# A decoder block's cross attention: all value and sum products of a batch in one row, and x2's turn in another bank

## The chip, the cores and the metric

The kernel runs on one NeuronCore of a Trainium2 chip. The metric is the device time of one execution in microseconds (us). The core has five engines, each with its own in-order instruction list: PE (TensorE, matrix products; PEld is its weight load), DVE (VectorE), ACT (ScalarE), POOL (GpSimd) and SP (SyncE, which issues transfers). They meet only at semaphores. Matrix products land in PSUM, a memory of eight banks.

## The reference

64 batches of 128 tokens with 128 features pass three parts, each followed by a residual sum and a layer norm. The change touches the second, cross attention to 77 context rows of 96 features, with 16 heads of 8:

```python
q = (x @ Wq).reshape(B, N, HEADS, hd).transpose(0, 2, 1, 3)
k = (context @ Wk).reshape(B, M, HEADS, hd).transpose(0, 2, 1, 3)
v = (context @ Wv).reshape(B, M, HEADS, hd).transpose(0, 2, 1, 3)
scores = jnp.einsum('bhid,bhjd->bhij', q, k) * scale
attn = jax.nn.softmax(jnp.where(mask, scores, max_neg), axis=-1)
out = jnp.einsum('bhij,bhjd->bhid', attn, v)
...
x = _layernorm(x + out.reshape(B, N, DIM) @ Wo, axis=-1)
```

Everything is float32.

## The kernel before

The program runs in stages, one behind the other: attention, cross attention (`attend_context`), gathering of expert slots, experts, mixing. In the profile cross attention lies between about 162 and 555 us. It goes in steps `n` from -1 to 67, one batch a step, and is pipelined by hand: in step `n` the scores of batch `n`, the products of batch `n - 2` with the values, the projection of batch `n - 3` and the turn of the finished x2 of batch `n - 4` are done. Each engine's list is written out in the loop `for n in STEPS` of its block, and nothing is reordered.

What a batch goes through:

- `own_keys` (POOL, L797) sets up its keys. `scores` (PE, L550) makes the scores of eight heads a half, in two halves that share the two banks of `psS`; `peak` (DVE, L701) takes their maxima. The second half's scores wait for the first half's peak.
- `turn_max` (PE, L530) turns the negative maxima into `psM`; ACT copies them to `mT` (L676). `turned_scores` (PE, L560) makes the scores again, with the context rows on the partitions, into the four banks of `psP`; `shift` (PE, L568) adds the maxima.
- `exponentials` (ACT, L641) reads `psP` in two halves, two banks each.
- `values` (PE, L579) and `sums` (PE, L585) multiply the exponentials with the values and with ones, both into `psO`, in column tiles of 32. Each comes in two parts, 16 instructions each.
- `invert_sums` (DVE, L720) takes the reciprocal of the sums, `divide` (L730) makes `oT`, `project` (PE, L535) multiplies with Wo into `psM`, `add_residual` (DVE, L708) makes y. Statistics (L710, L715), and `normalise` on POOL (L803 to L808), give x2 in `w.xres`.
- `turn_x2` (PE, L540) turns x2 into `psM`, ACT makes its high part (L679) and `low_part` (DVE, L724) the low one, which the next stage's logits use.

Beside these, every other step has `queries_keys` or `own_values` (PE, into `psM`) for a pair of batches, with their copies on ACT and `split_low` on DVE, and SP stores and reloads the packed queries and keys.

The bank `psM` is shared by five users. `take_bank(reader, count)` lets the next one begin when the reader of the one before is through: the list `held` keeps that semaphore. So after `project`, the next user waits for y (`y_done`).

Of the kernel before, what the change touches and what calls it, by code (L numbers as in the profile page):

```python
# [18 lines left out]
ALU = mybir.AluOpType  # L19
ACT = mybir.ActivationFunctionType  # L20
# [7 lines left out]
B, S, D = 64, 128, 128  # L28
TOKENS = B * S
J, JP, CD = 77, 78, 96  # L30
# [25 lines left out]
def reach(eng, sem, value):  # L56

    if not isinstance(value, int) or value > 0:
        eng.wait_ge(sem, value)  # L59
# [366 lines left out]
def attend_context(nc, io, w):  # L426
# [4 lines left out]
    with ExitStack() as ctx:  # L431
        st = Store(nc, ctx, "cross")
# [24 lines left out]
        qk_made, high_ready, low_ready, t_made = w.qk_made, w.high_ready, w.low_ready, w.t_made  # L457
        kd_ready, v_made, vd_ready = (st.sem(n) for n in ("kd_ready", "v_made", "vd_ready"))

        s_made, mx_ready, m_made, mT_ready, e_ready, av_made, rs_ready, oT_ready = (  # L460
            st.sem(n) for n in ("s_made", "mx_ready", "m_made", "mT_ready", "e_ready", "av_made", "rs_ready",
                                "oT_ready"))
# [6 lines left out]
        block = ctx.enter_context(nc.Block())  # L469
        PACKS = 6 * 16  # L470
        STEPS = range(-1, B + 4)

        def is_batch(n):
            return 0 <= n < B

        def projected(n):
            return [(n + 4) // 2] if n % 2 == 0 and 0 <= n + 4 < B else []
# [8 lines left out]
        def tokens(n):  # L486
            return slice(n * 128, n * 128 + 128)
# [18 lines left out]
        def _(pe):  # L506
            held = []

            def take_bank(reader, count):
                for sem, value in held:  # L510
                    pe.wait_ge(sem, value)
                held[:] = [(reader, count)]
# [23 lines left out]

            def turn_x2(n):
                pe.wait_ge(x2_kept, n + 1)
                take_bank(xl_ready, n + 1)
                pe.transpose(psM[:, 0:128], w.xres[:, tokens(n)], w.ident).then_inc(xT_made, 1)  # L540

            def scores(n, half):
                r, b = n // 2, n % 2
# [10 lines left out]
            def turned_scores(n):  # L554
                r, b = n // 2, n % 2
                reach(pe, e_ready, n)
                for q in range(4):
                    for i in range(4):
                        row = pack[r % 2][32 * i:32 * i + 32, q, :]
                        pe.matmul(psP[:, i, q, :], row[:, 256 + b * JP:256 + b * JP + J], row[:, b * 128:b * 128 + 128],  # L560
                                  start=(q == 0), stop=False, skip_group_check=True)
# [10 lines left out]
            def values(n, part):  # L572
                if part == 0:
                    pe.wait_ge(vd_ready, n // 2 + 1)
                    pe.wait_ge(e_ready, n + 1)
                    reach(pe, oT_ready, n)
                for i in range(2 * part, 2 * part + 2):
                    for q in range(4):
                        pe.matmul(psO[32 * q:32 * q + 32, 0, :], vd[n // 2 % 3][:, 4 * (n % 2) + q, 32 * i:32 * i + 32],  # L579
                                  pT[n % 2][:, i, q, :], start=(i == 0), stop=(i == 3), skip_group_check=True)  # L580
# [15 lines left out]

            for n in STEPS:
                if n == 2:
                    pe.wait_ge(od_set, 2)
                if is_batch(n):  # L600
                    scores(n, 0)
                for r in projected(n):
                    queries_keys(r)
                for r in valued(n):
                    own_values(r)
                if is_batch(n - 2):
                    values(n - 2, 0)
                if is_batch(n):
                    scores(n, 1)
                if is_batch(n - 2):  # L610
                    values(n - 2, 1)
                if is_batch(n - 3):
                    project(n - 3)
                if is_batch(n - 2):
                    sums(n - 2, 0)
                if is_batch(n):
                    turn_max(n)
                    turned_scores(n)
                if is_batch(n - 4):
                    turn_x2(n - 4)  # L620
                if is_batch(n - 2):
                    sums(n - 2, 1)
                if n == 0:
                    pe.wait_ge(consts_set, 1)
                if is_batch(n):
                    shift(n)
                if n == B:
                    turn_weights(0)
                    turn_weights(1)
                if n == B + 1:  # L630
                    turn_weights(2)
                    turn_weights(3)

        @block.scalar
        def _(act):
            def exponentials(n, half):
                if half == 0:
                    act.wait_ge(t_made, n + 1)
                    reach(act, av_made, n - 1)
                hs = slice(2 * half, 2 * half + 2)  # L640
                ins = act.activation(pT[n % 2][0:J, hs, :, :], psP[:, hs, :, :], ACT.Exp)  # L641
                if half == 1:
                    ins.then_inc(e_ready, 1)

            def weights_high(c):
                b = slice(c * 512, (c + 1) * 512)
                act.wait_ge(w_made, c + 1)
                act.copy(w.w1h[:, b], psW[:, b]).then_inc(wh_done, 1)

            for n in STEPS:  # L650
                if n in (1, 2):
                    act.wait_ge(pT_set, n)
                if n == B + 1:
                    weights_high(0)
                    weights_high(1)
                if n == B + 2:
                    weights_high(2)
                    weights_high(3)
                if is_batch(n - 1):
                    exponentials(n - 1, 0)  # L660
                for r in projected(n):
                    act.wait_ge(qk_made, r + 1)
                    reach(act, stored, 16 * r)
                    act.copy(qk[:, 0, :], psM[:, 0:WIDE]).then_inc(high_ready, 1)
                for r in valued(n):
                    act.wait_ge(v_made, r + 1)
                    act.wait_ge(vd_clear, min(r, 2) + 1)
                    reach(act, av_made, 2 * r - 4)
                    act.copy(blocks(vd[r % 3][0:J]), psM[0:J, 0:256].rearrange("j (c h e) -> j c h e", c=8, h=4))\
                        .then_inc(vd_ready, 1)  # L670
                if is_batch(n - 1):
                    exponentials(n - 1, 1)
                if is_batch(n):
                    act.wait_ge(m_made, n + 1)
                    reach(act, t_made, n)
                    act.copy(mT[:], psM[:, 0:128]).then_inc(mT_ready, 1)  # L676
                if is_batch(n - 4):
                    act.wait_ge(xT_made, n - 3)
                    act.copy(w.xh[0:127, tokens(n - 4)], psM[0:127, 0:128]).then_inc(xh_ready, 1)  # L679

        @block.vector
        def _(dve):
# [9 lines left out]
            def split_low(r):  # L692
                dve.wait_ge(high_ready, r + 1)
                dve.tensor_tensor(qk[:, 1, :], psM[:, 0:WIDE], qk[:, 0, :], ALU.subtract)\
                    .then_inc(low_ready, 1)
# [25 lines left out]

            def low_part(n):
                dve.wait_ge(xh_ready, n + 1)
                dve.tensor_tensor(w.xl[0:127, tokens(n)], psM[0:127, 0:128], w.xh[0:127, tokens(n)], ALU.subtract)\  # L724
                    .then_inc(xl_ready, 1)

            def divide(n):
# [16 lines left out]
            for n in STEPS:  # L744
                if n < 2:
                    clear_values(n + 1)
                if n == B + 3:
                    weights_low(2)
                if is_batch(n):
                    peak(n, 0)  # L750
                for r in projected(n):
                    split_low(r)
                if is_batch(n):
                    peak(n, 1)
                if is_batch(n - 3):
                    add_residual(n - 3)
                    aggregate(n - 3)
                if is_batch(n - 4):
                    low_part(n - 4)
                if n == B + 2:  # L760
                    weights_low(1)
                if is_batch(n - 2):
                    invert_sums(n - 2)
                    divide(n - 2)
                if n == B - 1:

                    dve.wait_ge(qk_made, PAIRS)
                    dve.wait_ge(w.phi_loaded, 32)
                    dve.tensor_copy(w.diff[:, :, 127], w.bias[:])
                    differences((0, 1))  # L770
                if n == B:
                    differences((2, 3))
                if n == B + 1:
                    weights_low(0)
                if n == B + 3:
                    weights_low(3)
# [694 lines left out]
```

## Time and profile before

| | |
|---|---|
| median of 3 runs | 1484.61 us (1484.57 to 1485.5) |
| span of the profiled execution | 1482.3 us, so the median lies 2.3 us above it |
| PE, PEld busy over the span | 92%, 74% |
| DVE, ACT, POOL busy over the span | 81%, 59%, 79% |
| mean granted TensorE clock | 0.976 of 2.4 GHz |

A profile is one execution. Busy shares are means over stages with different limits, and the ends of matmuls are modelled, so a PE that shows as busy can be waiting for part of that time. What a change in one stage is worth must be read from that stage's timeline.

### The profile page before, as it was taken

What the parts mean: (1) busy time and instruction counts of PE and PEld (TensorE: products, weight loads), DVE (VectorE), ACT (ScalarE), POOL (GpSimd) and SP (SyncE); (2) the same over time, 40 slices, a digit from 0 to 9 for tenths busy, and PEclk for the clock granted to TensorE, in tenths of its full rate; (3) what the DMA queues carried; (4) which work ended last, traced back from release to release, by engine and by line L of the source; (5) the groups of instructions that cost most, each with busy time, mean ns of one, the idle gap of its engine ahead of it and who ended that gap; (6) DMA issues with size and microseconds to landing.
All of it is one profiled execution on the core that took longest, in us unless ns stands there. A gap on an engine that the chain in (4) does not pass through costs nothing. (4 is left out here: it accounts for less than half of the span.)

```text
span 1482.3 us, 34966 instructions
## 1 busy us (share of the span) xinstructions
PE 1369.5 (92%) x12862; PEld 1092.1 (74%) x12862; DVE 1197.3 (81%) x2379; ACT 873.4 (59%) x1542; POOL 1167.6 (79%) x1036
## 2 busy tenths in 40 slices
PE   4765699999999977999999999996999999999998
PEld 3554566666666655777777777765999999999997
DVE  5998467766776766888888888886999999999996
ACT  2777444544544534777777777764566666666665
POOL 6344466666666645999999999995999999999997
PEclk8999599999999998999999999999999999999999
DMA  5110343333333305222222222212233233232231
GB/s 157 38 35 27 94 123 94 99 103 105 98 94 94 92 20 171 79 79 79 79 79 78 79 79 78 79 71 69 69 93 88 79 92 87 79 93 86 80 93 29
DMA packets 77195, 123.81 MB, mean 84 GB/s; under 512 B 8354, under 2 KB 45795, under 8 KB 77027
## 3 DMA queue, kind: packets, MB, share of 16 engines
q1 hardware_dynamic: 75426, 117.16, 25.2%
q0 software_dynamic: 1088, 4.19, 1.0%
q8 instruction: 104, 1.70, 0.5%
q14 instruction: 65, 0.52, 0.1%
q10 hardware_dynamic: 512, 0.23, 0.1%
HBM read 70.28 MB, written 51.27 MB: 82 GB/s over the span
## 5 line engine op out<-in xcount | busy, mean ns | idle before, releaser
L971 POOL TENSOR_TENSOR gather_d<-gather_e,gather_rinv 128x1024 f32<-128x1024 f32 x128 | 244.9, 1913 | 44.6 <-DVE gather_rinv L950 44.6
L1230 POOL TENSOR_TENSOR mix_c<-mix_e,mix_rinv 128x1024 f32<-128x1024 f32 x128 | 240.9, 1903 | 17.4 <-DVE mix_rinv L1218 13.4
L1298 PEld LDWEIGHTS last_Y<-kept_phi,last_cT 128*128 128x128 f32 x2048 | 248.3, 192 | 7.1
L1298 PE MATMUL last_Y<-kept_phi,last_cT 128*128 128x128 f32 x2048 | 249.1, 275 | 0.0
L1314 ACT COPY last_cT<-last_T 128x1024 f32<-128x1024 f32 x128 | 128.4, 1003 | 128.8 <-PE last_T L1305 128.8
L1215 DVE TENSOR_REDUCE mix_sums<-mix_e 128x16 f32<-128x1024 f32 x128 | 155.9, 1218 | 32.8 <-ACT mix_e L1189 32.6
L946 DVE TENSOR_REDUCE gather_rsum<-gather_e 128x32 f32<-128x1024 f32 x128 | 156.1, 1220 | 26.2 <-ACT gather_e L919 26.2
L797 POOL TENSOR_TENSOR cross_kd<-first_pack,kept_consts 128x624 fp32r<-128x624 f32 x128 | 155.5, 1236 | 18.9 <-DMA first_pack<-first_halves 12.5
L965 POOL TENSOR_TENSOR gather_dl<-gather_d,gather_dh 128x512 fp32r<-128x512 f32 x128 | 166.2, 1299 | 0.0
L641 ACT ACTIVATE cross_pT<-cross_P 77x1024 f32<-77x1024 f32 x128 | 130.3, 1021 | 49.7 <-PE cross_P L568 49.7
L908 ACT COPY gather_keep<-gather_L 128x256 f32<-128x256 f32 x256 | 94.7, 370 | 104.2 <-PE gather_L L882 97.2
L1305 PE MATMUL last_T<-kept_consts,mix_c 128*128 128x128 f32 x1024 | 133.8, 274 | 3.2 <-POOL mix_c L1230 1.2
L919 ACT ACTIVATE gather_e<-gather_L 128x1024 f32<-128x1024 f32 x128 | 131.1, 1025 | 7.8 <-PE gather_L L889 0.3
L896 PE MATMUL slots_X<-gather_d,kept_xres 128*128 128x512 f32 x256 | 130.7, 592 | 0.0
L1223 POOL TENSOR_TENSOR mix_less<-mix_read,mix_high 128x1024 f32<-128x1024 f32 x64 | 122.5, 1914 | 6.5 <-DVE mix_high L1205 3.7
L701 DVE TENSOR_REDUCE cross_mx<-cross_S 128x8 fp32r<-128x624 f32 x128 | 102.9, 804 | 28.7 <-PE cross_S L550 28.6
L1305 PEld LDWEIGHTS last_T<-kept_consts,mix_c 128*128 128x128 f32 x1024 | 113.8, 141 | 4.4 <-issue 2.5
L940 DVE TENSOR_REDUCE gather_mx<-gather_L 128x16 fp32r<-128x512 f32 x128 | 88.5, 691 | 31.7 <-PE gather_L L882 22.9
L901 PE MATMUL slots_X<-gather_dh,gather_x2h 128*128 128x512 f32 x128 | 101.0, 789 | 2.9 <-DVE gather_x2l L956 1.5
L803 POOL TENSOR_TENSOR cross_veps<-cross_mv,kept_eps 128x1 f32<-128x1 f32 x64 | 12.1, 190 | 110.0 <-DVE cross_mv L715 110.0
L931 ACT CAST gather_dh<-gather_d 128x512 fp32r<-128x512 f32 x128 | 79.5, 621 | 31.6 <-PE slots_X L903 20.1
L882 PE MATMUL gather_L<-over_w1h,kept_xh 128*128 128x512 f32 x256 | 82.0, 402 | 10.6 <-ACT gather_e L919 9.1
(195 smaller groups left out, 3166.2 us busy)
## 6 DMA issues: line engine op xcount, KB each, us to landing
kept_logits<-gather_keep SPq DMA_DIRECT2D x128, 256.0 KB, 2.0
mix_read<-kept_logits SPq DMA_DIRECT2D x64, 512.0 KB, 3.7
first_halves<-first_qk SPq DMA_DIRECT2D x32, 412.0 KB, 3.7
first_pack<-first_halves SPq DMA_DIRECT2D x64, 128.0 KB
first_pack<-first_halves SPq DMA_DIRECT2D x32, 206.0 KB
first_pack<-first_halves SPq DMA_DIRECT2D x64, 78.0 KB
attn_xTg<-in_xT SPq DMA_DIRECT2D x16, 256.0 KB, 2.8
kept_xres<-in_x POOLq DMA_DIRECT2D x4, 1024.0 KB, 12.8
```

What stands on the lines that cost most here:

```text
L641: ins = act.activation(pT[n % 2][0:J, hs, :, :], psP[:, hs, :, :], ACT.Exp)
L797: pool.tensor_tensor(kd[n % 2][:, q], keys[:, q].to_broadcast([128, 2, 4, JP]), w.own.unsqueeze(1).unsqueeze(3).to_broadcast([128, 2, 4, J ...
L896: pe.matmul(psX[:, 2 * j + 1, :], w.xres[:, rows(u)], dd[u % 4][:, 1, :], start=first, stop=last)\
L919: act.activation(e[u % 2][:], psL[u % 2][:].rearrange("p i (n s) -> p i n s", n=16), ACT.Exp)\
L946: dve.tensor_reduce(rsum[u % 2][:].rearrange("p (i n) -> p i n", i=2), e[u % 2][:], X, ALU.add)\
L965: pool.tensor_tensor(dl[u % 2][:], dd[u % 4][:, 0, :], dh[u % 2][:], ALU.subtract).then_inc(dl_ready, 1)
L971: pool.tensor_tensor(dd[u % 4][:].rearrange("p i (n s) -> p i n s", n=16), e[u % 2][:], rinv[u % 2][:].rearrange("p (i n) -> p i n", i=2). ...
L1215: dve.tensor_reduce(self.sums[u % 2][:], self.e[u % 2][:], X, ALU.add).then_inc(self.sum_done, 1)
L1230: pool.tensor_tensor(self.cc[u % 2][:], self.e[u % 2][:], self.rinv[u % 2][:].unsqueeze(2).to_broadcast([128, 16, EXPERTS]), ALU.mult)\
L1298: ins = pe.matmul(psY[t % 2][:, 0:128], cT[u % 2][:, c, :], w.yk[:, 8 * (u % 2) + c, :], start=(u % 2 == 0 and c == 0), stop=(u % 2 == 1 a ...
L1305: ins = pe.transpose(psT[:, c, :], mix.cc[u % 2][:, 2 * c:2 * c + 2, :], w.ident)
L1314: act.copy(cT[u % 2][:], psT[:]).then_inc(cT_ready, 1)
```

## The change

On PE, the two parts of the values and the two parts of the sums of batch `n - 2`, which stood at four places of a step, are issued in one row behind the second scores. The turn of x2 goes to the front of the step, ahead of the second scores. It writes the first bank of `psP` and not `psM`, for all but the last four batches, and waits for the first half of the exponentials (a new semaphore `e_low`); the turned scores, which write that bank, wait for the low part of x2. On ACT, x2's high part goes ahead of the second half of the exponentials. On DVE, the low part goes ahead of the second peak, and reciprocal and divide go ahead of the residual sum.

```diff
--- before.py
+++ after.py
@@ -457,6 +457,7 @@
         qk_made, high_ready, low_ready, t_made = w.qk_made, w.high_ready, w.low_ready, w.t_made
         kd_ready, v_made, vd_ready = (st.sem(n) for n in ("kd_ready", "v_made", "vd_ready"))
 
+        e_low = st.sem("e_low")
         s_made, mx_ready, m_made, mT_ready, e_ready, av_made, rs_ready, oT_ready = (
             st.sem(n) for n in ("s_made", "mx_ready", "m_made", "mT_ready", "e_ready", "av_made", "rs_ready",
                                 "oT_ready"))
@@ -469,9 +470,13 @@
         block = ctx.enter_context(nc.Block())
         PACKS = 6 * 16
         STEPS = range(-1, B + 4)
+        SHARED = B - 4
 
         def is_batch(n):
             return 0 <= n < B
+
+        def x2_turned(n):
+            return banks[:, 0, 0, :] if n < SHARED else psM[:, 0:128]
 
         def projected(n):
             return [(n + 4) // 2] if n % 2 == 0 and 0 <= n + 4 < B else []
@@ -536,8 +541,11 @@
 
             def turn_x2(n):
                 pe.wait_ge(x2_kept, n + 1)
-                take_bank(xl_ready, n + 1)
-                pe.transpose(psM[:, 0:128], w.xres[:, tokens(n)], w.ident).then_inc(xT_made, 1)
+                if n < SHARED:
+                    pe.wait_ge(e_low, n + 4)
+                else:
+                    take_bank(xl_ready, n + 1)
+                pe.transpose(x2_turned(n), w.xres[:, tokens(n)], w.ident).then_inc(xT_made, 1)
 
             def scores(n, half):
                 r, b = n // 2, n % 2
@@ -554,6 +562,7 @@
             def turned_scores(n):
                 r, b = n // 2, n % 2
                 reach(pe, e_ready, n)
+                reach(pe, xl_ready, n - 3)
                 for q in range(4):
                     for i in range(4):
                         row = pack[r % 2][32 * i:32 * i + 32, q, :]
@@ -603,23 +612,20 @@
                     queries_keys(r)
                 for r in valued(n):
                     own_values(r)
-                if is_batch(n - 2):
-                    values(n - 2, 0)
+                if is_batch(n - 4):
+                    turn_x2(n - 4)
                 if is_batch(n):
                     scores(n, 1)
                 if is_batch(n - 2):
+                    values(n - 2, 0)
                     values(n - 2, 1)
+                    sums(n - 2, 0)
+                    sums(n - 2, 1)
                 if is_batch(n - 3):
                     project(n - 3)
-                if is_batch(n - 2):
-                    sums(n - 2, 0)
                 if is_batch(n):
                     turn_max(n)
                     turned_scores(n)
-                if is_batch(n - 4):
-                    turn_x2(n - 4)
-                if is_batch(n - 2):
-                    sums(n - 2, 1)
                 if n == 0:
                     pe.wait_ge(consts_set, 1)
                 if is_batch(n):
@@ -638,9 +644,8 @@
                     act.wait_ge(t_made, n + 1)
                     reach(act, av_made, n - 1)
                 hs = slice(2 * half, 2 * half + 2)
-                ins = act.activation(pT[n % 2][0:J, hs, :, :], psP[:, hs, :, :], ACT.Exp)
-                if half == 1:
-                    ins.then_inc(e_ready, 1)
+                act.activation(pT[n % 2][0:J, hs, :, :], psP[:, hs, :, :], ACT.Exp)\
+                    .then_inc(e_ready if half == 1 else e_low, 1)
 
             def weights_high(c):
                 b = slice(c * 512, (c + 1) * 512)
@@ -668,15 +673,15 @@
                     reach(act, av_made, 2 * r - 4)
                     act.copy(blocks(vd[r % 3][0:J]), psM[0:J, 0:256].rearrange("j (c h e) -> j c h e", c=8, h=4))\
                         .then_inc(vd_ready, 1)
+                if is_batch(n - 4):
+                    act.wait_ge(xT_made, n - 3)
+                    act.copy(w.xh[0:127, tokens(n - 4)], x2_turned(n - 4)[0:127]).then_inc(xh_ready, 1)
                 if is_batch(n - 1):
                     exponentials(n - 1, 1)
                 if is_batch(n):
                     act.wait_ge(m_made, n + 1)
                     reach(act, t_made, n)
                     act.copy(mT[:], psM[:, 0:128]).then_inc(mT_ready, 1)
-                if is_batch(n - 4):
-                    act.wait_ge(xT_made, n - 3)
-                    act.copy(w.xh[0:127, tokens(n - 4)], psM[0:127, 0:128]).then_inc(xh_ready, 1)
 
         @block.vector
         def _(dve):
@@ -721,7 +726,7 @@
 
             def low_part(n):
                 dve.wait_ge(xh_ready, n + 1)
-                dve.tensor_tensor(w.xl[0:127, tokens(n)], psM[0:127, 0:128], w.xh[0:127, tokens(n)], ALU.subtract)\
+                dve.tensor_tensor(w.xl[0:127, tokens(n)], x2_turned(n)[0:127], w.xh[0:127, tokens(n)], ALU.subtract)\
                     .then_inc(xl_ready, 1)
 
             def divide(n):
@@ -750,18 +755,18 @@
                     peak(n, 0)
                 for r in projected(n):
                     split_low(r)
+                if is_batch(n - 4):
+                    low_part(n - 4)
                 if is_batch(n):
                     peak(n, 1)
+                if is_batch(n - 2):
+                    invert_sums(n - 2)
+                    divide(n - 2)
                 if is_batch(n - 3):
                     add_residual(n - 3)
                     aggregate(n - 3)
-                if is_batch(n - 4):
-                    low_part(n - 4)
                 if n == B + 2:
                     weights_low(1)
-                if is_batch(n - 2):
-                    invert_sums(n - 2)
-                    divide(n - 2)
                 if n == B - 1:
 
                     dve.wait_ge(qk_made, PAIRS)
```

## Rows read from the trace of the kernel before

**Rows 1.** Stretches: busy us (and instructions) by engine, granted clock, DMA share, GB/s

```profile
100.00:120.00 20.00, 13.09 (x90) 10.71 (x91) 19.02 (x70) 16.42 (x55) 8.64 (x9) 1.00 0.14 39
181.80:540.31 358.51, 348.44 (x6580) 243.38 (x6576) 249.46 (x576) 172.24 (x301) 238.09 (x303) 1.00 0.33 97
```

**Rows 2.** Timeline (start, us, engine): first and last regular shift

```profile
181.80 0.36 PEld L568 LDWEIGHTS cross_P<-cross_mT,cross_pick 32*77 32x77 f32 x16 [0.20 <-issue]
...
540.31 0.35 PEld L568 LDWEIGHTS cross_P<-cross_mT,cross_pick 32*77 32x77 f32 x16 [0.20 <-issue]
```

**Rows 3.** Timeline of one regular step, selected; idle time and releaser in brackets

```profile
451.50 0.38 PEld L585 LDWEIGHTS cross_O<-cross_pT,cross_od 128*32 128x32 f32 x16
...
452.08 0.36 PEld L568 LDWEIGHTS cross_P<-cross_mT,cross_pick 32*77 32x77 f32 x16 [0.20 <-issue]
...
452.22 0.96 DVE L720 RECIPROCAL cross_rs<-cross_O 128x128 f32<-128x128 f32 x1
452.51 0.30 PEld L550 LDWEIGHTS cross_S<-cross_kd,first_pack 128*128 128x128 f32 x2
...
452.63 1.02 ACT L641 ACTIVATE cross_pT<-cross_P 77x1024 f32<-77x1024 f32 x1 [0.75 <-PE cross_P L568]
...
453.21 0.29 DVE L730 TENSOR_TENSOR cross_oT<-cross_O,cross_rs 128x128 f32<-128x128 f32 x1
453.42 0.80 DVE L701 TENSOR_REDUCE cross_mx<-cross_S 128x8 fp32r<-128x624 f32 x1
...
453.62 0.41 PEld L579 LDWEIGHTS cross_O<-cross_pT,cross_vd 128*32 128x32 f32 x16 [0.35 <-issue]
...
454.33 0.30 PEld L550 LDWEIGHTS cross_S<-cross_kd,first_pack 128*128 128x128 f32 x2 [0.31 <-issue]
...
454.82 0.65 PE L579 MATMUL cross_O<-cross_pT,cross_vd 128*32 128x128 f32 x16
454.93 0.81 DVE L701 TENSOR_REDUCE cross_mx<-cross_S 128x8 fp32r<-128x624 f32 x1 [0.71 <-PE cross_S L550]
455.39 0.30 PEld L535 LDWEIGHTS cross_M<-first_xo,cross_oT 128*128 128x128 f32 x2 [0.20 <-issue]
...
455.92 0.29 DVE L708 TENSOR_TENSOR cross_y<-cross_M,kept_xres 128x128 f32<-128x128 f32 x1 [0.18 <-PE cross_M L535]
...
456.38 0.19 PEld L530 LDWEIGHTS cross_M<-kept_neg_ident,cross_mx 128*128 128x128 f32 x1 [0.20 <-issue]
...
456.64 0.36 PEld L560 LDWEIGHTS cross_P<-first_pack 32*77 32x77 f32 x16
...
456.75 0.27 ACT L676 CAST cross_mT<-cross_M 128x128 fp32r<-128x128 f32 x1 [1.92 <-PE cross_M L530]
...
457.13 0.14 PEld L540 LDWEIGHTS cross_M<-kept_consts,kept_xres 128*128 128x128 f32 x1
...
457.39 0.38 PEld L585 LDWEIGHTS cross_O<-cross_pT,cross_od 128*32 128x32 f32 x16
...
457.80 0.29 DVE L724 TENSOR_TENSOR kept_xl<-cross_M,kept_xh 127x128 fp32r<-127x128 f32 x1 [1.03 <-ACT kept_xh L679]
```

**Rows 4.** Timeline of the last steps and the next stage's first logits

```profile
541.84 0.84 PEld L579 LDWEIGHTS cross_O<-cross_pT,cross_vd 128*32 128x32 f32 x32 [1.18 <-issue]
541.87 1.08 PE L579 MATMUL cross_O<-cross_pT,cross_vd 128*32 128x128 f32 x32 [1.07 <-DVE cross_oT L730]
542.88 0.30 PEld L535 LDWEIGHTS cross_M<-first_xo,cross_oT 128*128 128x128 f32 x2 [0.20 <-issue]
...
551.12 0.29 DVE L708 TENSOR_TENSOR cross_y<-cross_M,kept_xres 128x128 f32<-128x128 f32 x1
...
551.52 0.14 PEld L540 LDWEIGHTS cross_M<-kept_consts,kept_xres 128*128 128x128 f32 x1 [0.64 <-issue]
...
553.82 0.14 PEld L540 LDWEIGHTS cross_M<-kept_consts,kept_xres 128*128 128x128 f32 x1 [2.16 <-POOL kept_xres L808]
...
555.65 0.50 PEld L882 LDWEIGHTS gather_L<-over_w1h,kept_xh 128*128 128x128 f32 x2 [1.69 <-issue]
```

## The prediction

> **What bounds the kernel now.** I looked for the stretch that the diff touches. The table by stretch gives it [rows 1]: from the first regular step to the last (181.80 to 540.31 us) TensorE is busy 348.44 of 358.51 us, at a granted clock of 1.00 (2.4 GHz), while VectorE has 249.46, GpSimd 238.09 and ScalarE 172.24. That looks like a TensorE bound, but the ends of matmuls are modelled. So I read the timeline next. The same instruction, the shift (L568), begins at 181.80 in step 2 and at 540.31 in step 63 [rows 2]: 358.51 / 61 = 5.877 us a step. A single step, from the sums at 451.50 to those at 457.39 [rows 3], takes 5.89, the same as this mean over steps whose lists differ (own_values in one, queries_keys in the next). That points to a loop of waits and not to the length of TensorE's list.
>
> The loop stands in the timeline of one step [rows 3]; follow the starts. Second half of the sums (451.50) to reciprocal (452.22): 0.72. Reciprocal to divide (453.21): 0.99. Divide to first peak (453.42): 0.21. Peak to second scores (454.33), which need the score bank that this peak reads: 0.91. Second scores, values, project, sums, turn of the maximum, turned scores, turn of x2, and the second half of the sums again (457.39): 0.49 + 0.57 + 0.99 + 0.26 + 0.49 + 0.26. Together 5.89, the period. So now the batch's reciprocal and divide stand between the sums and the next step's peak, and TensorE fills most of the time but waits a little for them.
>
> Note what does not stand in this loop: the residual sum y (455.92). It runs while the first half of the sums is on TensorE, so that the turn of the maximum, which needs y to have read bank M, finds the bank free at 456.38.
>
> **The change, part by part.** I write M for the start of the turn of the maximum and V for the start of the row of products.
>
> (a) *One row instead of four groups.* It removes no instruction. A group of 16 instructions costs 0.57 from start to the next kind (454.82 to 455.39), with 0.20 of idle weight load at its edge [rows 3]. Where the trace has 32 of them in a row, they take 1.08 against 0.65 for 16 (L579, matmul rows) [rows 3, 4], so a further 16 cost 0.43. Four groups of 0.57 are 2.28; one row is 0.57 + 3 x 0.43 = 1.86. TensorE's list gets 0.42 us shorter a step. Bounds for a further 16: 0.43 from the matmul rows, and 0.47 from the starts of the same run and of the project behind it (541.84 to 542.88, less 0.57); above, no saving at all, 0.57.
>
> The rule that supports this is in the Trainium skill, TensorEngine Tiling (Array Packing), "Tiling Modes": changing the tiling mode, not just the tile, drains the engine. The trace agrees, with the 0.20 us of idle weight load at such edges. By that rule alone fewer changes of mode make the kernel faster, to about 1451 us (rival 2); by VectorE's order, which comes next, it is 1544.
>
> (b) *The new order on VectorE.* It is now: first peak, split_low, low part, second peak, reciprocal, divide, then y of the batch before, stats. TensorE's order is: row, project, turn of the maximum. Project takes bank M, and the turn of the maximum may take it only when y has read it. But y is queued behind the reciprocal and the divide, and these wait for the end of the row. The reciprocal starts 0.72 after a group of 16 starts, so after a row V + 0.72 + 3 x 0.43 = V + 2.01. Then 0.99 to the divide, 0.21 to y (as the divide's follower starts now), 0.29 for y, and 0.11 from the end of a y to TensorE, as in the tail (551.12 + 0.29 to 551.52) [rows 4]. M = V + 3.61. TensorE has by then been done with the row and with project since V + 1.86 + 0.42 = V + 2.28. So it stands for 1.33 us, and turned scores, shift, and everything of the next step stand queued behind it. This is a wait that the kernel before does not have.
>
> (c) *x2's turn in the turned scores' first bank.* It now waits for the first half of the exponentials (e_low) and not for bank M. From M: the copy of the maximum on ScalarE starts 0.37 later and takes 0.27, plus 0.11 to TensorE: shift at M + 0.75 (turned scores, 0.26 + 0.49, are through at the same time). Shift to exponential: 452.08 to 452.63, 0.55; it takes 1.02; plus 0.11: the turn of x2 at M + 2.43. With 0.26 for itself (457.13 to 457.39), second scores at M + 2.69. The other road there goes by the peak: shift to first scores 0.43, scores to peak 0.60 (as from 454.33 to 454.93), peak 0.80, 0.11: M + 2.69. Both roads are equally long, so (c) costs nothing beside the peak; without that cover it would cost up to the difference to own_values' end (first scores to values is 1.11 at most, so M + 2.29), 0.4 us. The high and low copies come earlier in ScalarE's and VectorE's lists: x2's turn to the end of its low part is 0.96 (457.13 to 457.80 + 0.29), so M + 3.4. The next reciprocal is at M + 5.2, and in between lie only the second peak (0.8) and, every other step, split_low; no cost. The second exponential moves behind x's high copy, by 0.27, and is needed only at the next turned scores: no cost.
>
> (d) *Closing the loop.* Second scores to the next row: 0.49. V' = M + 3.18. Period = 3.61 + 3.18 = 6.79 us, against 5.877: +0.91 a step. GpSimd, DMA queues: own_keys and normalise sit where they were, the stores and packs of SP still hang on the shift; with longer steps each has more room. No cost.
>
> (e) *The ends.* Steps -1 to 1 hold nothing that moves. Step 2 has the row and no project, so no wait; it gains about 0.2. Steps 3 to 63 are 61 periods: 61 x 0.91 = 55.5. Behind the last shift, x2's turn now stands ahead of the row and of the project, so each of the last steps waits for the whole chain y, stats, GpSimd's normalise, which takes 2.70 from y to the turn of x2 (551.12 to 553.82) [rows 4]. From the shift S of step 63: y(60) at S - 1.15, turn at 1.55, row 1.81, reciprocal 3.82, y(61) 5.02, turn 7.72, row 7.98, reciprocal 9.99, y(62) 11.19, turn 13.89, low part done 14.85, project 15.0, y(63) 15.5, turn 18.2, next stage 20.0 (1.83 on, as from 553.82 to 555.65). Before it is 15.34 (540.31 to 555.65). +4.7.
>
> Sum: -0.2 + 55.5 + 4.7 = +60. What follows is not touched and is shifted as a whole. The profiled execution spans 1482.3, so 1542.3; the median of the runs lies 2.3 above the span, which gives 1544.6. I say 1544.
>
> **Rivals.**
>
> 1. *The row is not cheaper than its parts* (0.57 a group): reciprocal 0.42 later, period 7.21, 61 x 1.33 + 5 = +86, 1571. With 0.47 instead of 0.43 it is +0.12 a step, 1552. Against: the run of 32 in the tail.
>
> 2. *The other side: TensorE's list decides, y comes in time.* TensorE's starts in the new order: 0.26 + 0.49 + 0.43 + 1.11 + 0.26 + 0.49 + 1.86 + 0.42 = 5.32, so -0.56 a step, -34, about 1451. It holds if y is done within V + 2.28, that is if it is not behind reciprocal and divide, 1.2 us. The list puts it there, so I give this little. (It is the outcome that the Trainium skill's rule on drains, TensorEngine Tiling (Array Packing), "Tiling Modes", would lead one to expect.)
>
> 3. *The change does not show*: the new wait would have to be eaten by other slack to within 0.05 us a step. TensorE, busy 97% by the table, has no such slack on the road from M to V', which is a chain of ScalarE, VectorE and TensorE without gaps. 1485.
>
> 4. *The granted clock falls* to 1.2 GHz, because TensorE now stands 1.3 in 6.8 us. Against: a stretch of the attention stage keeps 1.00 with TensorE busy 13.09 of 20 us [rows 1], a smaller share than in the new step. At half the rate the row's 1.72 us (4 x 0.43) come again, and as an estimate 0.8 for the other matmuls on the loop (half of the 0.49 + 0.43 + 0.26 + 0.43 that they take there): 61 x 2.5 = 154 more, 1698.
>
> **How the numbers follow.** Forecast as worked out 0.86, alone between 1534 and 1557 (period 6.65 to 6.95, the latencies of 0.11 and the 0.43 each being good to some hundredths). Rival 1 with no saving 0.05, rival 2 0.04, rival 3 0.02, rival 4 0.03. About 0.2%, 3 us, is what a measurement of this kernel can tell. Slower 0.94, same 0.02, faster 0.04. The range for 8 in 10 is 1530 to 1562; it takes in the bound of 0.47 with something more.
>
> **What would show it.** After: the turn of the maximum begins about 6.8 us after its predecessor and each time about 0.11 after the end of y; y follows the divide at once; TensorE's longest idle time of a step, some 1.3 us, is put down to VectorE's y, ahead of L530; the reciprocal starts 2.0 after the row; the stage from the first to the last shift takes some 414 us in place of 358.5, with clock 1.00. If the period is 5.3 and y comes ahead of the reciprocal's end, I am wrong in (b); if x2's turn or second scores wait clearly beyond M + 2.7, in (c); if the reciprocal starts 2.4 after V, in (a).

## The result and the profile after

The changed kernel takes 1559.65 us (median of 4 runs, 1556.75 to 1562.27) against 1485.05 us: a ratio of 1.0503, 95% interval 1.0489 to 1.0517. It is 75 us slower; 59 had been forecast, and 1559.65 lies near the upper end of the range.

The profiled execution spans 1557.7 us, 75.4 more than before. The changed lines have moved by a few numbers: L535 is now the turn of the maximum, L577 the shift, L588 the values, L594 the sums, L540 project, L713 y, L725 the reciprocal, L548 x2's turn, L558 the scores. First the table by stretch (busy us and instructions of PE, PEld, DVE, ACT, POOL, then granted clock, DMA share, GB/s): from the turn of the maximum in step 2 to that in step 63, then the tail, then one long step.

```profile
179.02:601.86 422.84, 333.51 (x6579) 264.21 (x6576) 242.77 (x576) 169.26 (x301) 236.74 (x300) 0.96 0.27 82
601.86:627.82 25.96, 14.29 (x187) 11.39 (x188) 10.92 (x32) 5.51 (x11) 7.63 (x12) 0.67 0.00 1
...
480.18:489.30 9.12, 8.05 (x108) 6.42 (x108) 3.82 (x10) 2.74 (x5) 3.94 (x5) 0.63 0.13 47
```

Over the same 61 steps, counted there from shift to shift, TensorE was all but full before [rows 1]; now it is busy 333.51 of 422.84 us, and its clock is no longer 1.00. The timeline has the place: first and last regular shift, one regular step from the turn of the maximum to the next, the values of a long step, and the next stage's first logits.

```profile
179.71 0.35 PEld L577 LDWEIGHTS cross_P<-cross_mT,cross_pick 32*77 32x77 f32 x16
...
453.26 0.19 PEld L535 LDWEIGHTS cross_M<-kept_neg_ident,cross_mx 128*128 128x128 f32 x1 [1.44 <-issue]
...
453.62 0.27 ACT L684 CAST cross_mT<-cross_M 128x128 fp32r<-128x128 f32 x1 [3.12 <-PE cross_M L535]
...
453.94 0.35 PEld L577 LDWEIGHTS cross_P<-cross_mT,cross_pick 32*77 32x77 f32 x16
...
454.49 1.02 ACT L647 ACTIVATE cross_pT<-cross_P 77x1024 f32<-77x1024 f32 x1 [0.60 <-PE cross_P L577]
...
454.70 0.80 POOL L813 TENSOR_SCALAR kept_xres<-cross_y,cross_mv,cross_rstd 128x128 f32<-128x128 f32 x1
...
454.95 0.81 DVE L706 TENSOR_REDUCE cross_mx<-cross_S 128x8 fp32r<-128x624 f32 x1 [1.26 <-PE cross_S L558]
...
455.62 0.14 PEld L548 LDWEIGHTS cross_P<-kept_consts,kept_xres 128*128 128x128 f32 x1 [0.50 <-POOL kept_xres L813]
...
455.88 0.30 PEld L558 LDWEIGHTS cross_S<-cross_kd,first_pack 128*128 128x128 f32 x2
...
456.36 0.81 PEld L588 LDWEIGHTS cross_O<-cross_pT,cross_vd 128*32 128x32 f32 x32 [0.19 <-issue]
456.37 1.08 PE L588 MATMUL cross_O<-cross_pT,cross_vd 128*32 128x128 f32 x32
...
458.25 0.30 PEld L540 LDWEIGHTS cross_M<-first_xo,cross_oT 128*128 128x128 f32 x2 [0.20 <-issue]
...
458.39 0.96 DVE L725 RECIPROCAL cross_rs<-cross_O 128x128 f32<-128x128 f32 x1 [1.09 <-PE cross_O L594]
459.38 0.29 DVE L735 TENSOR_TENSOR cross_oT<-cross_O,cross_rs 128x128 f32<-128x128 f32 x1
459.59 0.28 DVE L713 TENSOR_TENSOR cross_y<-cross_M,kept_xres 128x128 f32<-128x128 f32 x1
...
459.98 0.19 PEld L535 LDWEIGHTS cross_M<-kept_neg_ident,cross_mx 128*128 128x128 f32 x1 [1.44 <-issue]
...
484.00 1.94 PE L588 MATMUL cross_O<-cross_pT,cross_vd 128*32 128x128 f32 x32
...
602.53 0.36 PEld L577 LDWEIGHTS cross_P<-cross_mT,cross_pick 32*77 32x77 f32 x16
...
627.82 0.50 PEld L887 LDWEIGHTS gather_L<-over_w1h,kept_xh 128*128 128x128 f32 x2 [1.79 <-issue]
```

The reader is to see three things. The turn of the maximum (459.98) begins 0.11 us after the end of y (459.59 + 0.28), with 1.44 us of idle weight load ahead of it, while project had begun at 458.25. Y begins behind the divide (459.38), the divide behind the reciprocal (458.39). In the kernel before [rows 3], y lay between the two halves of the sums and the reciprocal behind it. Last, the 32 value products of the step with the turn at 480.18 take 1.94 us (484.00), those of the regular step 1.08 (456.37): the long step ran in part at the lower of the two clock levels, with 0.63 on the mean.

Where the 75.4 us are, from the starts of the shift and of the next stage:

| part | before | after | difference |
|---|---|---|---|
| to the shift of step 2 | 181.80 | 179.71 | -2.1 |
| 61 steps, before at their mean of 5.877, after at their median of 6.73 | 358.5 | 410.5 | +52.0 |
| what some steps take above that | 0 | 12.3 | +12.3 |
| last shift to the next stage's logits | 15.34 | 25.29 | +10.0 |
| the stages behind | 926.65 | 929.88 | +3.2 |

### The profile page after: what moved, and what is told of

Same layout as the page of the kernel before. It is cut to its first block and busy times, and to the rows that moved or that the text cites. A ratio compares the mean times of both kernels' runs of the same rounds, so it can differ in the third digit from the quotient of the medians.

```text
span 1557.7 us, 35026 instructions
## 1 busy us (share of the span) xinstructions
PE 1362.8 (87%) x12862; PEld 1121.5 (72%) x12862; DVE 1188.6 (76%) x2379; ACT 870.1 (56%) x1542; POOL 1168.4 (75%) x1036
## 5 line engine op out<-in xcount | busy, mean ns | idle before, releaser
L684 ACT CAST cross_mT<-cross_M 128x128 fp32r<-128x128 f32 x64 | 17.0, 265 | 203.8 <-PE cross_M L535 203.8
L725 DVE RECIPROCAL cross_rs<-cross_O 128x128 f32<-128x128 f32 x64 | 61.3, 958 | 67.6 <-PE cross_O L594 67.6
```

## The experiments

Step lengths are the distances between the starts of the turn of the maximum. "Long" are steps above 7.4 us.

```
kernel           median step   what steps take above it   time us    ratio to before (95%)
before           5.88          -0.5                       1485.05    1
after            6.73          12.3 (8 long)              1559.65    1.0503 (1.0489 to 1.0517)
e1_y_first       5.93           6.0 (4 long)              1499.12    1.0097 (1.0068 to 1.0125)
e2_project_mid   5.55           0.1                       1465.97    0.9873 (0.9858 to 0.9887)
e3_fill          6.73           3.6 (2 long)              1548.67    1.0428 (1.0412 to 1.0444)
e4_x2_back       7.05 to 8.66, in turn                    1601.81    1.0772 (1.0737 to 1.0807)
e5_x2_alone      5.56           0.6                       1467.87    0.9893 (0.9877 to 0.9910)
e6_fill10        6.73           0.7 (0 long)              1545.21    1.0410 (1.0392 to 1.0428)
e7_ahead         5.29           3.2 (1 long)              1451.75    0.9779 (0.9760 to 0.9797)
e8_row_alone     5.88          -1.0                       1484.78    0.9999 (0.9990 to 1.0008)
```

**e1_y_first: y ahead of the reciprocal.** One edit to the changed kernel, on VectorE:

```diff
-                if is_batch(n - 2):
-                    invert_sums(n - 2)
-                    divide(n - 2)
                 if is_batch(n - 3):
                     add_residual(n - 3)
                     aggregate(n - 3)
+                if is_batch(n - 2):
+                    invert_sums(n - 2)
+                    divide(n - 2)
```

> One edit to the changed kernel: on VectorE the residual sum y and its statistics stand ahead of reciprocal and divide again. Theory A (y queued behind reciprocal and divide is the new wait): y starts 2.4 us after the row, with project, in place of 3.2; the turn of the maximum 2.8 after the row in place of 3.6; the period falls from 6.73 to about 5.9 us and the total to some 1495 us. Theory B (the row itself, or x2's turn in the other bank, is what makes the step longer): the period stays near 6.7 us and the total near 1558 us.

Measured: 1499.12 us, 5.93 us a step. In its timeline the row begins at 450.62, y at 453.03, 2.41 behind it, and the turn of the maximum at 453.44, 2.82 behind it.

```profile
450.62 0.81 PEld L588 LDWEIGHTS cross_O<-cross_pT,cross_vd 128*32 128x32 f32 x32 [0.19 <-issue]
...
452.50 0.30 PEld L540 LDWEIGHTS cross_M<-first_xo,cross_oT 128*128 128x128 f32 x2 [0.20 <-issue]
...
453.03 0.29 DVE L713 TENSOR_TENSOR cross_y<-cross_M,kept_xres 128x128 f32<-128x128 f32 x1 [1.09 <-PE cross_M L540]
...
453.44 0.19 PEld L535 LDWEIGHTS cross_M<-kept_neg_ident,cross_mx 128*128 128x128 f32 x1 [0.64 <-issue]
...
453.79 0.94 DVE L725 RECIPROCAL cross_rs<-cross_O 128x128 f32<-128x128 f32 x1
```

The reciprocal (453.79) now comes after the turn of the maximum. Theory A holds: the place of the residual sum in VectorE's list was worth 60 of the 75 us, the long steps that went with it among them.

**e2_project_mid: y under the sums.** As e1, and on TensorE:

```diff
                     values(n - 2, 1)
-                    sums(n - 2, 0)
-                    sums(n - 2, 1)
                 if is_batch(n - 3):
                     project(n - 3)
+                if is_batch(n - 2):
+                    sums(n - 2, 0)
+                    sums(n - 2, 1)
```

> As e1, and project goes between the values and the sums of the row, so that y is read while the sums run. Theory A: no wait for y is left; the turn of the maximum comes 2.4 us after the row's start, right behind the sums; period about 5.5 us, total about 1472 us, faster than the kernel before. Theory B: near 6.7 us a step still, total near 1560 us.

Measured: 1465.97 us, 5.55 us a step, 1.3% faster than the kernel before. Its timeline, from one row of values to the next:

```profile
449.58 0.81 PEld L588 LDWEIGHTS cross_O<-cross_pT,cross_vd 128*32 128x32 f32 x32 [0.19 <-issue]
...
450.59 0.30 PEld L540 LDWEIGHTS cross_M<-first_xo,cross_oT 128*128 128x128 f32 x2 [0.20 <-issue]
...
451.00 0.81 PEld L594 LDWEIGHTS cross_O<-cross_pT,cross_od 128*32 128x32 f32 x32
...
451.12 0.29 DVE L714 TENSOR_TENSOR cross_y<-cross_M,kept_xres 128x128 f32<-128x128 f32 x1 [0.61 <-PE cross_M L540]
...
452.02 0.19 PEld L535 LDWEIGHTS cross_M<-kept_neg_ident,cross_mx 128*128 128x128 f32 x1 [0.20 <-issue]
...
452.15 0.96 DVE L726 RECIPROCAL cross_rs<-cross_O 128x128 f32<-128x128 f32 x1 [0.20 <-PE cross_O L594]
...
455.13 0.81 PEld L588 LDWEIGHTS cross_O<-cross_pT,cross_vd 128*32 128x32 f32 x32 [0.19 <-issue]
```

Project starts at 450.59, y at 451.12 while the sums (451.00) run, and the turn of the maximum at 452.02, 2.44 behind the row's start, finds bank M free.

**e4_x2_back, e5_x2_alone, e8_row_alone: the two halves of the change.** E4 undoes x2's move in the changed kernel. E5 makes this move alone in the kernel before. E8 has the row alone, in e2's order, that is with project between values and sums, so that the row is two groups of 32.

```diff
# e5: x2's turn in the kernel before
+                if is_batch(n - 4) and n - 4 < SHARED:
+                    turn_x2(n - 4)
                 if is_batch(n):
                     scores(n, 1)
...
                     turned_scores(n)
-                if is_batch(n - 4):
+                if n - 4 >= SHARED and is_batch(n - 4):
                     turn_x2(n - 4)
# e4 and e8: x2's turn back in bank M, behind the turned scores
-                if is_batch(n - 4):
-                    turn_x2(n - 4)
                 if is_batch(n):
                     scores(n, 1)
...
                     turned_scores(n)
+                if is_batch(n - 4):
+                    turn_x2(n - 4)
```

> The changed kernel with x2's turn alone undone: bank M, behind the turned scores, its copies last in ScalarE's and VectorE's lists; the row stays. If x2's move costs nothing, as predicted, and only takes x2's turn (0.26 us) from between turned scores and shift: the period grows to about 7.0 us, total about 1577 us. If x2's move is part of what made the kernel slower: the period falls below 6.7 us, total under 1555 us.

Measured: 1601.81 us. For most of the stage the steps come in turn, as about 8.6, 8.05, 7.05 and 7.05 us; those at full clock are 7.05, 0.32 longer than in the changed kernel. So x2's move saves 0.32 us a step there. The rest of the loss goes with the clock: 0.87 over the regular steps, the lowest of all these kernels.

```profile
180.00:647.04 467.04, 367.67 (x6474) 290.02 (x6471) 243.71 (x566) 169.66 (x296) 235.10 (x297) 0.87 0.25 74
```

> The kernel before with x2's move alone: its turn goes into the turned scores' first bank, between the first values and the second scores, with its copies earlier on ScalarE and VectorE; values and sums stay in four groups, VectorE keeps y ahead of the reciprocal. If the loop sums, reciprocal, divide, peak, second scores sets the step, as read from the trace of before, it loses x2's 0.26 us between turned scores and the second sums and may get back 0.12 before the second scores: period 5.6 to 5.75 us, total 1469 to 1477 us. If x2's move costs as much as it saves: 1485 us.

Measured: 1467.87 us, 5.56 us a step. x2's move alone makes the kernel before 1.1% faster, 0.32 us a step, a little more than expected. In its timeline the loop of the kernel before is still there, without x2's 0.26 us, and the second half of the sums starts 0.43 behind the turned scores (451.36 to 451.79), where x2's turn had started 0.49 behind them.

> The row without x2's move, and without the wait for y: values, project, sums behind both scores; y ahead of reciprocal and divide; x2's turn in bank M behind the turned scores, as in the kernel before, only its low part is made last on VectorE. With e5_x2_alone it tells the two halves of the change apart. If the row's saving of some 0.4 us of TensorE is hidden, because the loop of waits and not TensorE's list sets the step: e2's 5.55 us plus the 0.32 us that x2's move was worth in e4, 5.85 to 5.9 us a step, total 1482 to 1488 us. If the row saves its 0.4 us: about 5.5 us a step, total 1463 us.

Measured: 1484.78 us, 5.88 us a step, ratio 0.9999 (0.9990 to 1.0008). Together the three give a table of four: neither 5.88, x2's move alone 5.56, the row alone 5.88, both (e2) 5.55. So the row, taken by itself and without the wait for y, gains nothing. The timeline of e8, from one row to the next, shows what became of it:

```profile
446.36 0.81 PEld L587 LDWEIGHTS cross_O<-cross_pT,cross_vd 128*32 128x32 f32 x32 [0.18 <-issue]
...
447.37 0.30 PEld L540 LDWEIGHTS cross_M<-first_xo,cross_oT 128*128 128x128 f32 x2 [0.20 <-issue]
...
447.79 0.81 PEld L593 LDWEIGHTS cross_O<-cross_pT,cross_od 128*32 128x32 f32 x32
...
448.80 0.19 PEld L535 LDWEIGHTS cross_M<-kept_neg_ident,cross_mx 128*128 128x128 f32 x1 [0.20 <-issue]
...
449.93 0.29 DVE L735 TENSOR_TENSOR cross_oT<-cross_O,cross_rs 128x128 f32<-128x128 f32 x1
...
450.23 0.30 PEld L558 LDWEIGHTS cross_S<-cross_kd,first_pack 128*128 128x128 f32 x2
...
450.82 0.81 DVE L706 TENSOR_REDUCE cross_mx<-cross_S 128x8 fp32r<-128x624 f32 x1 [0.32 <-PE cross_S L558]
...
451.75 0.30 PEld L558 LDWEIGHTS cross_S<-cross_kd,first_pack 128*128 128x128 f32 x2 [0.76 <-issue]
...
452.23 0.81 PEld L587 LDWEIGHTS cross_O<-cross_pT,cross_vd 128*32 128x32 f32 x32 [0.19 <-issue]
```

The values take 1.01 us (446.36 to 447.37) and the sums 1.01 (447.79 to 448.80), 2.02 us for what was four groups of 0.57 [rows 3]: TensorE's list is 0.26 us shorter. (The row in one piece, in the changed kernel, takes 1.89: 456.36 to 458.25.) But the step now has another loop than the kernel before. The divide is through at 450.22 (449.93 + 0.29), and the first peak (450.82) waits for the first scores (450.23) and no longer for the divide. From row to row the loop is: values, project and sums 2.44, from the turn of the maximum over turned scores, x2's turn and shift to the first scores 1.43, to the peak 0.59, to the second scores 0.93, to the row 0.48, together 5.87. So the new order takes reciprocal and divide off the loop, and lays the first half of the values, the shift and the first scores on it. The shorter list counts on this loop, but the longer road uses it up. That the old loop and the new one come to the same 5.88 us is a coincidence, and so is 5.56 beside 5.55: in e2 it is the new loop without x2's turn, in e5 the old one without it.

**e3_fill and e6_fill10: the clock.** The changed kernel, with work added where TensorE waits for y (six products in e3, ten in e6; their output is overwritten):

```diff
                     project(n - 3)
+                    if is_batch(n):
+                        pe.wait_ge(mx_ready, 2 * n + 2)
+                        for q in (0, 1, 0, 1, 0, 1):
+                            pe.matmul(psS[:, q, 0:HW], w.neg_ident[:], pick[:].rearrange("p q t -> p (q t)"),
+                                      start=True, stop=True)
```

> The changed kernel with six added products of constants (128x128 by 128x312, some 0.9 us) into the score banks in the time in which TensorE stands for y. They are extra work that the next scores overwrite. Theory C (the ten steps that take 7 to 9 us in place of 6.73, and the slow last steps, come from the granted clock falling because TensorE stands 1.4 us in each step): the period stays 6.73 us, the long steps are gone, the clock stays 1.00 between the first and last step, and the total falls by 12 to 18 us to about 1543 us. Theory D (they come from something else, a transfer or the batches' pairs): the long steps stay, total 1560 us or more.

> As e3_fill, with ten added products instead of six, which fill the wait for y up to some 0.15 us. Theory C (the clock falls because TensorE stands in each step): the long steps, ten without filling and four with six products, go to none or one; period still 6.73 us; total near 1545 us. Theory D: the number of long steps does not follow the filling and stays at four or more.

Measured: 1548.67 and 1545.21 us, with the same 6.73 us a step. The long steps go from eight to two to none. Two of the ten that the expectations count, of 6.96 us, stay in all three kernels 128 to 129 us apart, at a clock of 1.00 (255.42:262.38 in the changed kernel), so they have another cause, which stays open. The regular steps of e3, by stretch:

```profile
180.03:594.15 414.12, 375.83 (x6945) 303.87 (x6941) 242.56 (x576) 169.52 (x301) 237.03 (x300) 0.99 0.28 84
```

and of e6:

```profile
181.19:592.39 411.20, 398.87 (x7189) 336.06 (x7185) 242.60 (x576) 169.21 (x301) 236.81 (x300) 1.00 0.28 85
```

More work on TensorE, and 14 us less time: theory C holds for the long steps. The products cost nothing since they stand where TensorE stood anyway.

**e7_ahead: one step further.** As e2, with x2's turn beside project, its copies behind the second exponentials and behind the statistics, and

```diff
-                if is_batch(n):
-                    scores(n, 0)
...
                     sums(n - 2, 1)
+                if is_batch(n + 1):
+                    scores(n + 1, 0)
                 if is_batch(n):
                     turn_max(n)
```

> As e2_project_mid, with two more edits: x2's turn stands beside project between values and sums, and the next batch's first scores are issued behind the sums, ahead of the turn of the maximum, so that their peak and the exponentials are off the road to the second scores. If TensorE's own list bounds e2 by now (starts of its pieces add up to 5.4 to 5.6 us), the period falls only to about 5.45 and the total to about 1460 us. If e2 is still bound by the road over exponentials, peak and normalise (3.1 us from the turn of the maximum to the row), the period falls to 5.2 or less, total 1445 us.

Measured: 1451.75 us, 2.2% faster than the kernel before and the fastest here; 5.29 us a step lies between the two expectations, nearer to the second. In its timeline

```profile
449.62 0.96 DVE L726 RECIPROCAL cross_rs<-cross_O 128x128 f32<-128x128 f32 x1
...
450.61 0.29 DVE L736 TENSOR_TENSOR cross_oT<-cross_O,cross_rs 128x128 f32<-128x128 f32 x1
450.82 0.80 DVE L707 TENSOR_REDUCE cross_mx<-cross_S 128x8 fp32r<-128x624 f32 x1
...
451.73 0.30 PEld L558 LDWEIGHTS cross_S<-cross_kd,first_pack 128*128 128x128 f32 x2 [0.43 <-issue]
...
452.21 0.81 PEld L588 LDWEIGHTS cross_O<-cross_pT,cross_vd 128*32 128x32 f32 x32 [0.18 <-issue]
```

reciprocal, divide and first peak stand end to end, and the second scores (451.73) still wait for the peak (450.82 + 0.80), 0.43 us of idle weight load: reciprocal, divide and peak are on the loop again, as in the kernel before [rows 3]. That reading comes from this one timeline; no run took it apart further. The one long step (from 197.47, 9.21 us at a mean clock of 0.84) is of another kind: in it ScalarE's copy of the queries and keys waits 2.59 us for a store, and project has 2.82 us of idle weight load ahead of it.

## Why the prediction was right, and by how much it was off

The wait that the prediction named is there, and the total lies within its range. That it does is in part luck: the range was meant for some hundredths of a us in each step, and there the steps came out 3.5 us below the forecast (52.0 against 55.5). The total lies above the forecast because of the long steps and the tail, where the clock fell, and the sum had that at nothing.

**(b), the new wait, was right.** Shown by e1 and e2. Its terms, forecast and measured from the timeline of after: row to reciprocal 2.01, 2.03; to divide 0.99, 0.99; to y 0.21, 0.21; y's start to the turn of the maximum 0.40, 0.39.

**(c) and (d), the road back to the row, were right to some hundredths.** Turn of the maximum to shift 0.75, measured 0.68; to x2's turn 2.43, measured 2.36; x2's turn to the second scores 0.26, 0.26; these to the row 0.49, 0.48. The period comes to 6.72, against 6.79. One road was left out of (c): x2's turn also waits for GpSimd's normalise of the y of the step before, which ends at 455.50 (454.70 + 0.80), while the first half of the exponentials ends at 455.51. It was a tie, so the sum did not suffer. What (c) called free was more than that: e4 and e5 show that x2's move is a gain of 0.32 us a step, in the changed kernel and in the one before. The prediction had taken x2's 0.26 us off the road to the shift, but never set it down as a gain of its own.

**(a), the row, was right in its size.** 1.89 us, forecast 1.86. The trace agrees with the rule on drains in the Trainium skill, TensorEngine Tiling (Array Packing), "Tiling Modes": with fewer changes of mode TensorE's list is 0.39 us shorter a step (four times 0.57, less 1.89). In the changed kernel this counts, since the reciprocal waits for the row's end. Against the kernel before, the row is worth nothing, as e8 shows, because its order makes a loop just as long. That also answers rival 2: e2 and e8 have no wait for y, and neither comes to the 5.32 us that TensorE's list alone would give. Rivals 1 and 3 fell with the row's 1.89 us and the ratio of 1.0503.

**(e), the ends, was mis-sized.** Forecast +4.7 behind the last shift, measured +10.0. The chain y, normalise, x2's turn is there, but two of its links are longer than in the steps from which they were taken. The rows below are from the tail of the changed kernel, the first a stretch as in the table of the result.

```profile
605.33:608.90 3.57, 3.57 (x65) 2.99 (x65) 0.29 (x1) 1.18 (x2) 0.00 (x0) 0.50 0.02 5
...
602.37 0.63 POOL L808 TENSOR_TENSOR cross_veps<-cross_mv,kept_eps 128x1 f32<-128x1 f32 x1 [7.36 <-DVE cross_mv L720]
...
603.08 0.89 POOL L811 TENSOR_TENSOR cross_rstd<-cross_veps,kept_neg_half 128x1 f32<-128x1 f32 x1
...
605.33 1.94 PE L588 MATMUL cross_O<-cross_pT,cross_vd 128*32 128x128 f32 x32
...
609.04 0.96 DVE L725 RECIPROCAL cross_rs<-cross_O 128x128 f32<-128x128 f32 x1 [3.01 <-PE cross_O L594]
```

The first row runs at a clock of 0.50, and the reciprocal starts 3.71 us behind it (605.33 to 609.04); the second, at 0.57, takes 3.33 (613.87 to 617.20). The forecast had 2.01 for each, so 3.0 us of the missing 5.3 are here. GpSimd's two small steps ahead of the normalise take 1.52 us (0.63 + 0.89) in the first round and 1.43 in the second, against 0.75 in a regular step: another 1.4 us, whose cause no run shows. Step 2 gained 0.34 us (from the turn of the maximum in step 1 to the shift of step 2, 7.45 before and 7.11 after) where 0.2 was forecast. The rest of the -2.1 in the table is there before the first step: the same weight load of `own_values` starts at 162.00 before and at 160.26 after.

**Rival 4 was set aside for a poor reason, and part of it came true.** The steps' surplus of 12.3 us is the largest piece that the forecast of +59 lacks. I had argued with a stretch of the attention stage that keeps 1.00 with TensorE busy 13.09 of 20 us [rows 1]. After the change TensorE is busy 333.51 of 422.84 us, a larger share than that, and the granted clock falls all the same, to between 0.62 and 0.79 in eight of 61 steps, so the argument did not hold. The clock of 1.00 and the 414 us that were to show the forecast are 0.96 and 422.8. E3 and e6 show that filling the wait takes the long steps away. The Trainium skill, TensorE: Matmul & The Clock Gate, "A second HAM failure mode: psum-queue depth-cycling", tells of a kernel in which TensorE idles for short times between groups of products so often that its clock goes back and forth between the two levels. The trace agrees in kind, with pauses of about 1.3 us and 0.63 in the long step at 480.18. What sets off a long step stays open: e1, with 0.64 us of idle weight load ahead of the turn of the maximum, still has four long steps, e2 none.

The stages behind, +3.2: the experts' stage, which the diff doesn't touch, has 33.4 us at a mean clock of 0.80 against 30.3 at 0.94. It has 32.9 at 0.81 in e2, 31.1 at 0.89 in e6 and 30.4 at 0.94 in e4, so it follows neither the row nor the wait for y; its cause stays open.

## What to carry to other kernels

When work is moved on one engine, write down for each engine what now stands ahead of the instruction that frees the shared buffer; here a residual sum of 0.29 us, put behind a reciprocal that waits for a long row, cost 0.80 us in each of 61 steps (6.73 against 5.93). A new order on an engine can shorten its list and gain nothing, because it makes another loop of waits that is just as long, as the row alone did: find the loop, write it out again for the new order, and take instructions off it, as x2's move did. And count a new pause on TensorE more than once, since the clock may fall with it.

## What the runs showed of the hardware

Ten added products a step made the kernel 14 us faster (1559.65 to 1545.21), with the granted clock at 1.00 over the regular steps instead of 0.96 and the long steps gone. In e4, where TensorE is busy 367.67 of 467.04 us, the clock falls in a regular pattern: from the turn of the maximum at 456.26 steps of 8.57 us at 0.80, 8.05 at 0.79 and two of about 7.05 at 1.00, over and over. The stretch of the attention stage that keeps 1.00 has TensorE busy a smaller part of the time [rows 1].
